# Attention of a post-norm transformer layer: R two and AV four stages behind the scores, AV issued first, five E buffers

## The reference

```
q = x @ q_w.T                       # 16 heads of 64
k, v = split(x @ kv_w.T)            # one key/value head of 64 for all
# windows of 256 tokens, each by itself
a = softmax(q k.T / 8)              # 256 x 256 per head and window
o = a v
x = layernorm(x + o @ proj_w.T + proj_b)
h = silu(x @ wg.T) * (x @ wu.T)     # 3072 hidden, int8 weights * 1/127
x = layernorm(x + h @ wd.T)
```

## Time and profile before

| | |
|---|---|
| median of 3 runs | 967.46 us (967.39 to 974.69) |
| the profiled execution | 966.28 us |
| its span, slowest core (core 5) | 964.5 us |
| spans of the cores | 954.9 to 964.5 us |
| PE busy | 802.2 us (83%) |
| DVE busy | 304.1 us (32%) |
| ACT busy | 195.4 us (20%) |

### The profile page before, as it was taken

How to read it: one execution, slowest core, us unless ns; L and a number is a source line. 1 busy time by engine, 2 the same in 40 slices (tenths; PEclk the granted TensorE clock), 3 DMA queues, 4 the chain that set the end, 5 groups by cost and what they waited for, 6 DMA issues and landing times.

```text
span 964.5 us, 11053 instructions; the slowest of 8 cores (954.9 to 964.5 us)
## 1 busy us (share of the span) xinstructions
PE 802.2 (83%) x3872; PEld 335.0 (35%) x3872; DVE 304.1 (32%) x410; ACT 195.4 (20%) x361; POOL 124.8 (13%) x247
## 2 busy tenths in 40 slices
PE   3657777758989999958888899777898999999996
PEld 3122223223434444412333333332343444443332
DVE  0146675332121222113444454533212122211111
ACT  0033332222121111102222222322212111111111
POOL 4000010002212223300000010000221223310000
PEclk8567777798999999967999999787899999999999
DMA  8970120224434445371111131132443445521121
GB/s 103 241 184 13 22 56 1 98 78 151 143 109 142 131 149 155 105 122 44 44 45 44 45 88 33 45 99 86 146 139 111 141 142 153 153 87 54 67 68 63
DMA packets 47173, 94.05 MB, mean 98 GB/s; under 512 B 5776, under 2 KB 5776, under 8 KB 47120
## 3 DMA queue, kind: packets, MB, share of 16 engines
q0 software_dynamic: 37744, 67.91, 27.6%
q1 hardware_dynamic: 9376, 25.43, 8.2%
HBM read 63.44 MB, written 12.58 MB: 79 GB/s over the span
## 4 chain that ended last, share of the span: by engine, by line
PE 62%; DMA 12%; DVE 12%; issue 7%; ACT 5%; POOL 1%; SPq 0%; DVEq 0%; ACTq 0%; POOLq 0%
PE ps L265 62%; DMA wqsb<-wq 6%; DMA x<-xtm 5%; DVE pool L369 5%; ACT r L698 2%; DVE r L690 2%; DVE silu L690 2%; DMA xbf<-xfm 1%; ACT silu L698 1%; DVE x2s L708 1%; DVE pool L321 1%; DVE xbf L434 1%; DVE hbuf L572 1%; DMA wuw<-wu 0%; ACT lnst L702 0%
## 5 line engine op out<-in xcount | busy, mean ns | idle before, releaser
L265 PE MATMUL ps<-xbf,wuw 128*128 128x512 bf16 x768 | 187.0, 388 | 11.3 <-DVE hbuf L572 11.0
L265 PE MATMUL ps<-xbf,wgw 128*128 128x512 bf16 x768 | 185.8, 386 | 12.2 <-DVE xbf L434 12.2
L265 PE MATMUL ps<-wdres,hbuf 128*128 128x512 bf16 x768 | 189.5, 393 | 7.6 <-PE ps L265 0.3
L572 DVE SCALAR_TENSOR_TENSOR hbuf<-ps,silu 128x512 bf16<-128x512 f32 x96 | 66.4, 692 | 270.8 <-PE ps L265 266.5
L369 DVE RECIPROCAL pool<-ps 128x256 f32<-128x256 f32 x64 | 112.4, 1757 | 64.1 <-PE ps L265 63.6
L567 ACT ACTIVATE silu<-ps 128x512 f32<-128x512 f32 x96 | 56.9, 597 | 278.4 <-PE ps L265 278.4
L265 PEld LDWEIGHTS ps<-xbf,wuw 128*128 128x128 bf16 x768 | 75.9, 99 | 107.0 <-issue 20.7
L265 PEld LDWEIGHTS ps<-xbf,wgw 128*128 128x128 bf16 x768 | 75.6, 99 | 106.8 <-issue 21.3
L265 PEld LDWEIGHTS ps<-wdres,hbuf 128*128 128x128 bf16 x768 | 71.2, 100 | 115.3 <-issue 46.9
L350 ACT ACTIVATE pool<-ps 128x512 bf16<-128x512 f32 x128 | 74.9, 596 | 154.5 <-PE ps L265 144.7
L542 POOL DMA_DIRECT2D wgw<-wg x96 | 50.8, 529 | 335.7 <-PE ps L265 335.7
(11 more groups left out here) (51 smaller groups left out, 255.0 us busy)
## 6 DMA issues: line engine op xcount, KB each, us to landing
wgw<-wg POOLq DMA_DIRECT2D x96, 256.0 KB, 2.6
wuw<-wu POOLq DMA_DIRECT2D x96, 256.0 KB, 2.6
x<-xtm SPq DMA_DIRECT2D x16, 512.0 KB, 3.7
y<-x SPq DMA_DIRECT2D x16, 512.0 KB, 2.9
wdres<-wd POOLq DMA_DIRECT2D x1, 6144.0 KB, 50.0
wqsb<-wq POOLq DMA_DIRECT2D x18, 256.0 KB, 4.2
xbf<-xfm POOLq DMA_DIRECT2D x16, 256.0 KB, 13.1
x2scr<-x2s SPq DMA_DIRECT2D x16, 256.0 KB, 2.1
```

The source lines that it names most:

```text
L265: last = t.matmul(o, l, r, start=st_, stop=sp, tile_position=tpos)
L572: return v.scalar_tensor_tensor(H_sb[:, m, n * 512:(n + 1) * 512], bank(6)[:, 0:512], FS, silu_sb[:, par, n * 512:(n + 1) * 512], ALU.mult ...
```

## The change

R runs two stages behind S instead of one, and AV four instead of two. In a stage AV is emitted ahead of R. E gets five slots, for which `rr` moves up in the pool and the matrix of ones moves into a buffer of its own. A chain now has four stages without S, and all four are handed to the projection: the first ahead of projection tile 0 (which needs the O of step 28), the second to fourth where the first and second were, and behind the layer norm of tile 1.

```diff
-        E3_v = pap[:, 10240:13312].rearrange("p (e x) -> p e x", e=3)
-        rr_v = pap[:, 13312:14336].bitcast(F32).rearrange(
+        E3_v = pap[:, 10240:15360].rearrange("p (e x) -> p e x", e=5)
+        rr_v = pap[:, 15360:16384].bitcast(F32).rearrange(
             "p (a w) -> p a w", a=2)
-        ones64_v = pap[:, 14336:14400]
+        ones64_v = sb("ones64", [128, 64], BF16)[:, :]
...
-            e3 = (j * NBLK + b) % 3
+            e3 = (j * NBLK + b) % 5
...
-            for i in range(NCH + 2):
+            for i in range(NCH + 4):
...
-                    if 1 <= i <= NCH:
-                        j, b = divmod(i - 1, NBLK)
-                        emit_rrep(j, b)
+                    if 4 <= i <= NCH + 3:
+                        j, b = divmod(i - 4, NBLK)
+                        emit_AV(j, b)
                     if 2 <= i <= NCH + 1:
                         j, b = divmod(i - 2, NBLK)
-                        emit_AV(j, b)
+                        emit_rrep(j, b)
...
         def emit_projseg(st, drain=()):
+            if drain:
+                drain[0]()
             emit_proj_mm(st, 0)
             fin0 = emit_proj_lnspill(st, 0, 0, scratch="silu", defer=True)
-            if drain:
-                drain[0]()
+            if len(drain) > 1:
+                drain[1]()
             fin0()
             emit_proj_mm(st, 1)
             fin1 = emit_proj_lnspill(st, 1, 1, scratch="silu", defer=True)
-            if len(drain) > 1:
-                drain[1]()
+            if len(drain) > 2:
+                drain[2]()
             fin1()
-            for f in drain[2:]:
+            for f in drain[3:]:
                 f()
...
-            tail = stages[-2:]
-            stages = stages[:-2]
+            tail = stages[-4:]
+            stages = stages[:-4]
...
-        for f in stages0[:-2]:
+        for f in stages0[:-4]:
             f()
-        drain = stages0[-2:]
+        drain = stages0[-4:]
```

## The result

The changed kernel takes 980.16 us in the median, the kernel before 967.54; the ratio of the two is 1.0129, with a 95% interval of 1.0093 to 1.0165, so it is slower by about 12.5 us. The profiled execution took 978.17 us, its spans are 968.8 to 976.4 us over the cores (954.9 to 964.5 before), and the mean granted clock of a core is 0.891 to 0.895 against 0.886 to 0.898.

A forecast was written before the change was run, and what follows sets the result against it. No engine is saturated; the loop through bank 7 between R and the reciprocal sets the pace. Terms 5.2 + 4.7 + 0.8 + 0 - 1.0 + 0 = +9.7 us give 977.2 us, range 969 to 983.

The forecast's parts named there:

- Part 1: Two chain tails: one more turn through bank 7 before the projection, 2.6 us each, 5.2 us in all.
- Parts 2 and 3: AV before R: shared-stage query halves lose 10 x 0.47 = 4.7 us; six steps behind a layer norm, 0.8 us.
- Part 4: Steady solo pairs: a later reciprocal and an earlier query half cancel, net 0 for seven pairs, bounds -2 and +2 us.
- Part 5: Filling: first stages of each chain have fewer matmuls, -0.25 us in the first supertile, some -0.8 in the second.
- Part 6: Drain inside the projection: AV31 waits for its normalisation and holds tile 2, 0 us, bounds 0 and +1.5 each.
- B: Additions hide and only the tails show: +4.2 us, 971.7 us; chance 0.20.
- C: Faster: AV ahead of R keeps PE's clock high in solo pairs and slow shared steps, -15 us, 952 us; chance 0.05.
- D: Slower: the longer wait takes the clock from the second query half too, 12 us more, 989 us; chance 0.13.

The follow-up runs named there:

- the last four runs: R given two banks in the solo chain: kernel before 0.9947, changed kernel 0.9951, and the same two with three rr slots 0.9932 and 0.9855.
- e9: Kernel before, but in the solo chain R alternates between banks 6 and 7 and both query halves use bank 5: ratio 0.9947.
- e12: Changed kernel with R alternating between banks 6 and 7 in the solo chain, query halves in bank 5, three rr slots: ratio 0.9855, 951.9 us.

## Why the prediction was right, point by point

The forecast was 977.2 us, the range 969 to 983; measured were 980.2. The direction, the places and most sizes hold. The reason given for the tails does not, and that its size came out is partly luck.

- **Part 1, the tails.** Forecast 2.6 us each, measured 2.9 and 2.7. But the reason was only half right. I counted R's on PE and blamed drain stage 32 ahead of tile 0. The runs with the distance alone and with R30 behind tile 0 show that it is the reciprocal of step 29, behind which the normalisation of step 28 stands; R's distance alone adds the turn (+2.8 and +2.4 us). The step that failed here is the path: tile 0 is held through VectorE's queue, not through the number of R's on PE.
- **Parts 2 and 3, AV ahead of R in the shared stage.** Forecast 4.7 + 0.8 = 5.5, measured 6.1 us, and 5.8 to 6.8 at the same clock. The query half waits 0.50 where I had 0.47. The reciprocal stands 0.53 behind the normalisation where I had 0.36 + 0.11, since the normalisation took 0.42. Behind a layer norm the step was mis-sized: I let the down unit follow R after 0.38 us, it follows after 0.57 (478.03 to 478.60), and the stretch is 0.38 us longer instead of 0.13. By the runs at the same clock the order alone costs 3.8, the own-engine wait 3.2 to 3.5 and the distance 0.4 at most; that adds up to the whole within 0.8 us.
- **Part 4, solo pairs.** Forecast 0 for the steady pairs, and from the fifth on they take 13.6 to 13.7 us before and 13.6 to 13.8 after. I had set 0.47 against a saving of 0.60 in which the query half follows R after 0.40; it follows after 0.57 and saves 0.43, and the two still cancel. The stretch as a whole is +2.1, just over the bound of +2: 1.0 from the pair at the high level that three cores had before and none has after, which the sum didn't count, and 1.2 in the early pairs, whose cause is open.
- **Part 5, filling.** Forecast -0.25 and -0.8, measured 0 in the first chain and -0.9 in the second.
- **Part 6, the drain.** Forecast 0 with AV31 held; measured held for 6.80 us, covered, and moving it gained nothing. The +0.3 and +0.7 us from tile 1 to tile 2 are not its doing.
- **Rivals.** B (only the tails) is out by the 13.3 us of idle time on the reciprocal. C (the clock rises) is out for this kernel: no pair of it has both query halves at 1.9 us. D's size is out too, since from the second pair on every pair has one slow half and no more; but a pair at the high level, which three cores had before, none has after. C's mechanism is real: one pair had it on three cores of the kernel before, and all pairs from the second on once R had two banks with the changed order.

The first section of the prediction said that the distance buys nothing that PE waits for today. That holds, and the last four runs show what it rests on: the loop through R's bank. The same section said that a turn costs the same after the change, which it does (2.72 us).

## What to carry to other kernels

Before lengthening a software pipeline, find the loop that sets its pace, here one PSUM bank that was written, read and written again; a longer distance can pay only when that loop is open, and here nearly all that it then paid came through the clock. At the end of the chain, count the extra steps on the engine that is slow and holds the last result in its queue, not on the one that issues. Look at which slots a reordering makes neighbours on one engine: a third slot of 1 KB per partition gave back 3.3 us of the shared stage. And compare a stage between kernels on cores with the same granted clock in that stage: the order alone seemed to cost 1.9 us by the means and cost 3.8.

## What the runs showed of the hardware that I had not expected

- A wait on the instruction just ahead on VectorE, a reciprocal behind a normalisation, costs 0.18 us (0.53 against 0.34 to 0.35 us from start to start).
- At the low clock a group of 128x512 matmuls follows R (64 output columns per tile) after 0.57 us, AV follows it after 0.40 (160.04 to 160.44).
- The granted clock of the solo stretch was 0.72 in e9, where PE is busy 19.5 of 24 us with 123 matmuls, and 1.00 in e12, where it is busy 17.1 of 24 us with 138. I had given the clock's help a chance of 0.05.
- In one execution of the kernel before, the second solo pair took 11.5 us at a granted clock of 1.00 on three cores and 13.5 to 13.8 us at 0.75 on the other five.
